# A split-float32 gated MLP with top-k masking on one Trainium2 core: the second of four token blocks takes the seven-product form of the shared down projection, and GpSimd multiplies by the magnitudes earlier

## The reference, cut to what matters

```python
xn = layernorm(x)                                   # x: 4 x 512 tokens of 1024 features
# part 1: gated MLP, 2752 units, half of them set to zero for each token
s = silu(xn @ w_gate.T)                             # 2752 columns
s = where(|s| is among the k = 1376 smallest of its row, 0, s)
part1 = (s * (xn @ w_up.T)) @ w_down.T
# part 2: squared-ReLU MLP ("shared", 2048 units) and one linear path ("routed", 512)
h = relu(xn @ up_w) ** 2
shared = h @ down_w                                 # 2048 -> 1024
routed = ((xn @ fc1_w) @ expert_w) * (sum of the 2 largest of xn @ gate_w) @ fc2_w
y = x + part1 + layernorm(shared + routed) * ln_gamma + ln_beta
```

## Time and profile before

| | us |
|---|---|
| median of 3 runs | 2283.11 (2279.87 to 2283.51) |
| profiled execution, its own time | 2282.36 |
| span of that execution's instructions | 2280.1 |
| TensorE busy in the span | 2263.9 (99%) |
| VectorE, ScalarE, GpSimd busy | 1327.3, 751.3, 939.2 |
| mean share of the DMA engines, from 637.07 MB | 79.9% |

### The profile page before, as it was taken

The page is one execution under the profiler, slowest core; times in us unless marked ns, Lnnn a source line. Parts: engine busy times, 40 slices in busy tenths (PEclk is TensorE's granted clock), DMA queues, the critical chain, the costliest instruction groups (busy, mean ns, idle before and its releaser), DMA issues.

```text
span 2280.1 us, 27377 instructions
## 1 busy us (share of the span) xinstructions
PE 2263.9 (99%) x10264; PEld 1882.5 (83%) x10264; DVE 1327.3 (58%) x1712; ACT 751.3 (33%) x1173; POOL 939.2 (41%) x670
## 2 busy tenths in 40 slices
PE   8999999999999999999999999999999999999999
PEld 6888888888888888888888888888788888888877
DVE  4332678757334456937434446788943543888870
ACT  3233654133334325301114334623112432551310
POOL 5456557487444523044014461136403455043620
PEclk9999999999999999999999999999999999999999
DMA  6799999788888878887678887668677888676955
GB/s 257 278 389 395 354 366 354 264 341 299 292 297 280 273 278 312 295 292 289 213 233 296 272 278 284 213 228 288 239 251 248 268 283 309 216 231 226 333 186 177
DMA packets 229158, 637.07 MB, mean 279 GB/s; under 512 B 23712, under 2 KB 32928, under 8 KB 225952
## 3 DMA queue, kind: packets, MB, share of 16 engines
q1 hardware_dynamic: 229024, 635.30, 79.9%
HBM read 483.10 MB, written 152.11 MB: 279 GB/s over the span
## 4 chain that ended last, share of the span: by engine, by line
PE 92%; DVE 3%; DMA 2%; SPq 1%; POOL 1%; ACT 1%; issue 0%; DVEq 0%; ACTq 0%
PE bank L1330 30%; PE bank L1332 30%; PE bank L1331 30%; PE bank L1350 1%; DMA mixed_w<-mixes 1%; DVE prod L1925 1%; DMA split_w<-w 1%; PE bank L1341 1%; SPq L800 0%; POOL w L1061 0%; SPq L796 0%; DVE prod_t L2061 0%; DVEq L1491 0%; PE bank L1430 0%; PE bank L1431 0%
## 5 line engine op out<-in xcount | busy, mean ns | idle before, releaser
L1061 POOL TENSOR_TENSOR w<-raw,w 128x512 fp32r<-128x512 f32 (+1 forms) x196 | 282.3, 1447 | 195.0 <-ACT w L1107 194.6
L1066 POOL TENSOR_TENSOR w<-w 128x512 fp32r<-128x512 f32 x146 | 214.5, 1496 | 199.1 <-ACT w L1284 199.0
L1330 PE MATMUL bank<-w,prod_t 128*128 128x512 f32 x672 | 269.5, 401 | 3.0 <-DVE prod_t L2061 3.0
L1332 PE MATMUL bank<-w,prod_t 128*128 128x512 f32 x672 | 262.9, 391 | 0.0
L1331 PE MATMUL bank<-w,prod_t 128*128 128x512 f32 x672 | 261.9, 390 | 0.0
L1330 PE MATMUL bank<-w,tok 128*128 128x512 f32 (+1 forms) x664 | 252.8, 381 | 0.7 <-ACT mag L1218 0.5
L1331 PE MATMUL bank<-w,tok 128*128 128x512 f32 (+1 forms) x664 | 252.0, 380 | 0.0
L1332 PE MATMUL bank<-w,tok 128*128 128x512 f32 (+1 forms) x664 | 252.0, 379 | 0.0
L1330 PE MATMUL bank<-tok,w 128*128 128x512 f32 x640 | 249.0, 389 | 0.0
L1331 PE MATMUL bank<-tok,w 128*128 128x512 f32 x640 | 249.0, 389 | 0.0
L1332 PE MATMUL bank<-tok,w 128*128 128x512 f32 x640 | 249.0, 389 | 0.0
(11 more groups left out here) (222 smaller groups left out, 4633.7 us busy)
## 6 DMA issues: line engine op xcount, KB each, us to landing
w<-split_w SPq DMA_DIRECT2D x448, 512.0 KB, 4.5
split_w<-w SPq DMA_DIRECT2D x184, 512.0 KB, 6.2
w<-mixed_w SPq DMA_DIRECT2D x176, 256.0 KB, 3.2
w_more<-split_w SPq DMA_DIRECT2D x88, 512.0 KB, 5.1
w_more<-mixed_w SPq DMA_DIRECT2D x128, 256.0 KB, 3.7
rows<-x_dram SPq DMA_DIRECT2D x32, 512.0 KB, 5.0
mixed_w<-own SPq DMA_DIRECT2D x12, 1024.0 KB, 6.8
spilled_u<-prod SPq DMA_DIRECT2D x12, 1024.0 KB, 8.0
```

The lines of the kernel that those rows point to most:

```text
L1061: pool.tensor_tensor(lo, words, hi, ALU.subtract).then_inc(lo_ready, 1)
L1066: pool.tensor_tensor(slot_of(g)[:, 1, :], slot_of(g)[:, 1, :].bitcast(F32), slot_of(g)[:, 0, :], ALU.subtract).then_inc(pool_lo, 1)
L1330: pe.matmul(out, left[0], right[0], start=first, stop=False)
L1332: return pe.matmul(out, left[1], right[0], start=False, stop=last)
```

## The change

It does three things. (1) `WIDE` becomes true for block 1, which so takes the order of a wide block and the seven-product form for pairs 5 and 6. (2) The eight sets of these pairs are made elsewhere: sets 20 to 23 in block 0 by VectorE, in a new buffer `first_own` over the search's scratch (loads from granules 148, 158, 176 and 192, mixing at +7, store at +8), and sets 24 to 27 in block 1 by GpSimd in `shared_own` (two loads at a granule and two at the next, from 152, 158, 165 and 172; mixing at +3; store at +5). (3) In wide blocks GpSimd multiplies chunks 0 to 15 of `prod` by `mag` before they are spilled (granules 148 to 151, four instructions of 128x2048), in place of sixteen of 128x512 behind out 0's masks; TensorE's turns then wait for the mask itself. The spills stand at 151, 153, 155 and 157.

```diff
-WIDE = [False, False, True, True]
+WIDE = [False, True, True, True]
...
+            if wide:
+                self.spill_at = {second + 4 + 2 * c: c for c in range(4)}
+                self.weigh_at = {second + 1 + c: c for c in range(4)}
...
         if wide:
-            for c in range(6):
-                del self.gated_at[out0 - TURN_LEAD + c]
+            self.gated_at = {}
             self.gated_at.update({begun + 6 + c: c for c in range(6)})
...
-SHARED_FROM = {n: 158 + 7 * i for i, n in enumerate(SHARED_SETS)}
-SHARED_LOADS = {at + i: (n, i) for n, at in SHARED_FROM.items() for i in range(4)}
-SHARED_AT = {at + 5: n for n, at in SHARED_FROM.items()}
-SHARED_STORES = {at + 6: n for n, at in SHARED_FROM.items()}
+FIRST_SHARED, SECOND_SHARED = SHARED_SETS[:HALF], SHARED_SETS[HALF:]
+SHARED_FROM = [dict(zip(FIRST_SHARED, (148, 158, 176, 192))), dict(zip(SECOND_SHARED, (152, 158, 165, 172)))]
+SHARED_LOADS = [{at + i: [(n, i)] for n, at in SHARED_FROM[0].items() for i in range(4)},
+                {at + i: [(n, 2 * i), (n, 2 * i + 1)] for n, at in SHARED_FROM[1].items() for i in range(2)}]
+SHARED_AT = [{at + 7: n for n, at in SHARED_FROM[0].items()}, {at + 3: n for n, at in SHARED_FROM[1].items()}]
+SHARED_STORES = [{at + 8: n for n, at in SHARED_FROM[0].items()}, {at + 5: n for n, at in SHARED_FROM[1].items()}]
...
+        first_own = over("first_own", [P, 4, N], F32, more_at + 2 * HID * 4)
...
             def load_shared_mix(n, i):
-                if n > SHARED_SETS[0]:
+                if n == FIRST_SHARED[0]:
+                    sp.wait_ge(masked, TILES)
+                elif n != SECOND_SHARED[0]:
                     sp.wait_ge(shared_stored, 16 * (n - SHARED_SETS[0]))
...
             def spill(b, c):
-                sp.wait_ge(up_signed, SIGNED.index((b, c)) + 1)
+                if WIDE[b]:
+                    sp.wait_ge(weighed, weighings(b, c) + 1)
+                else:
+                    sp.wait_ge(up_signed, SIGNED.index((b, c)) + 1)
...
+            def mix_second_shared(n):
+                ...                                  # the four subtractions, on GpSimd
...
+                    if m in plan.weigh_at:
+                        c = plan.weigh_at[m]
+                        ks = slice(4 * c, 4 * c + 4)
+                        pool.wait_ge(up_signed, SIGNED.index((b, c)) + 1)
+                        pool.tensor_tensor(prod[:, ks, :, :], prod[:, ks, :, :], mag[:, ks, :, :],
+                                           ALU.mult).then_inc(weighed, 1)
...
             def upper_early_sum(b, n):
                 act.wait_ge(unit_summed, shared_round(b, n) * UNIT_SUMS + 1)
+                if b == 1 and n == 0:
+                    act.wait_ge(shared_stored, 16 * len(SHARED_SETS))
...
             def turn_product(b, i):
-                pe.wait_ge(prod_ready, b * GK + i + 1)
+                if WIDE[b] and i >= TAIL_CHUNKS:
+                    pe.wait_ge(masked, (b * GC + GROUPS.index(c // 4) + 1) * TILES)
+                else:
+                    pe.wait_ge(prod_ready, prods(b, i) + 1)
```

More of the change, by code:

```diff
@@ L171, in __init__ @@
         self.late_hi_at, self.units_lo_at, self.units_cut_at = {}, {}, {}
+        self.weigh_at = {}
         shared_end = end["fast", SHARED_PAIRS[1], 6] if wide else end[("shared", 3)]
@@ L513, in unit_lo, with weighings, prods @@
     return len(names) * shared_round(b, n) + names.index(what) + 1
+def weighings(b, c):
+    return 4 * WIDE[:b].count(True) + c
+def prods(b, i):
+    return sum(TAIL_CHUNKS if wide else GK for wide in WIDE[:b]) + i
+TAIL_CHUNKS = 6
 SIGNED = [(b, g) for b in range(1, BLOCKS) for g in (GC - 2, 0, 1, 2, 3)]
@@ L724, in program @@
         prod_ready = sem("prod_ready")
+        weighed = sem("weighed")
         norm_step = sem("norm_step")
@@ L776, in late_place, with shared_place @@
             return raw_more[:, i, :]
+        def shared_place(n):
+            return first_own if n in FIRST_SHARED else shared_own
         def results_of(name):
@@ L841, in load_shared_mix @@
                 src, width = words_of((PAIRS[p][i // 2], k + i % 2 * HALF))
-                sp.dma_start(shared_own[:, i, :], src).then_inc(shared_loaded, 16)
+                sp.dma_start(shared_place(n)[:, i, :], src).then_inc(shared_loaded, 16)
             def store_shared_mix(n):
                 sp.wait_ge(shared_mixes, 4 * (n - SHARED_SETS[0]) + 4)
-                sp.dma_start(mixed_w[n].rearrange("i p n -> p i n"), shared_own[:, :, :]).then_inc(shared_stored, 16)
+                sp.dma_start(mixed_w[n].rearrange("i p n -> p i n"), shared_place(n)[:, :, :]).then_inc(shared_stored, 16)
             def load_norm(b):
@@ L870, in load_slot @@
                     sp.wait_ge(apply_step, b * 4 * TILES)
+                    if b == 1:
+                        sp.wait_ge(shared_stored, 16 * len(FIRST_SHARED))
                 for n, p in enumerate(SHARED_PAIRS):
@@ L931, in other_loads @@
                     store_own_mix(OWN_STORES[m])
[L932 to L935, removed]
+                if b < 2:
+                    for n, i in SHARED_LOADS[b].get(m, []):
+                        load_shared_mix(n, i)
+                    if m in SHARED_STORES[b]:
+                        store_shared_mix(SHARED_STORES[b][m])
                 if m == (plan.norm_load if b else FIRST_NORM_LOAD):
@@ L1033, in lower_early @@
                                    ALU.subtract).then_inc(early_lo, 1)
+            def mix_second_shared(n):
+                b11, b21, b12, b22 = (shared_own[:, i, :] for i in range(4))
+                at = 4 * (n - SHARED_SETS[0])
+                pool.wait_ge(shared_loaded, 64 * (n - SHARED_SETS[0] + 1))
+                pool.tensor_tensor(b11, b12, b11, ALU.subtract).then_inc(shared_mixes, 1)
+                pool.tensor_tensor(b12, b22, b12, ALU.subtract).then_inc(shared_mixes, 1)
+                pool.wait_ge(shared_mixes, at + 1)
+                pool.tensor_tensor(b22, b22, b11, ALU.subtract).then_inc(shared_mixes, 1)
+                pool.wait_ge(shared_mixes, at + 3)
+                pool.tensor_tensor(b21, b21, b22, ALU.subtract).then_inc(shared_mixes, 1)
             def late_mix(n):
@@ L1070, in _ @@
                             sum_lo(b, SUMS_LO_AT[b][m], j)
+                    if b == 1 and m in SHARED_AT[1]:
+                        mix_second_shared(SHARED_AT[1][m])
                     if m in plan.units_lo_at:
@@ L1564, in mix_own, with mix_first_shared @@
                 dve.tensor_tensor(b21, b21, b22, ALU.subtract).then_inc(own_mixes, 1)
-            def mix_shared(n):
-                b11, b21, b12, b22 = (shared_own[:, i, :] for i in range(4))
+            def mix_first_shared(n):
+                b11, b21, b12, b22 = (first_own[:, i, :] for i in range(4))
                 at = 4 * (n - SHARED_SETS[0])
@@ L1991, in _ @@
                                           ALU.subtract).then_inc(vector_lo, 1)
-                    if b == 1 and m in SHARED_AT:
-                        mix_shared(SHARED_AT[m])
+                    if b == 0 and m in SHARED_AT[0]:
+                        mix_first_shared(SHARED_AT[0][m])
                     if m in plan.units_at:
```

## The result

The changed kernel takes 2288.24 us (median of 10 runs, 2285.1 to 2289.93) against 2281.83 before (10 runs, 2279.87 to 2286.73): ratio 1.0028, 95% interval 1.002 to 1.0036, slower by 0.28%. The forecast was 2286.5, with 2277 to 2292 as the range. The profiled execution took 2289.93 us, the longest of the ten, with a span of 2288.1; so the differences of the traces come to 8.0 us where the medians differ by 6.4. By the line that the prediction drew (above 2287.7) this is slower.

A forecast was written before the change was run, and what follows sets the result against it. TensorE, busy 2263.9 of 2280.1 us, was taken as the bound. Terms -8.2 - 5.1 + 13.2 + 3.5 = +3.4 us took the profiled 2282.36 to 2285.8, or 2286.5 with 0.75 to the median; range 2277 to 2292.

The forecast's parts named there:

- Part 1: Block 1 in the wide form: 48 fewer matmuls make it as short as block 2, own waits apart; -8.2 us.
- Part 2: Products ahead of the spill: both waits in out 0 go, 1.7 us in each of three wide blocks; -5.1 us.
- Part 3: Block 1: ScalarE's wait for set 27's store delays count, pick, `cut_units` and A12; +13.2 us, within 11.9 and 15.
- The steps behind the store: Block 1, after set 27's store goes: landing, `upper_early_sum` (1.0 us), count (2.7 later), then the pick (7.1).
- So 1472.2 to 1475; I take 1473.5: Block 1, in block 2's times: when set 27's store goes, at some 17.5 us a set against 19.0 scheduled.
- Part 4: Block 0: the moved sets' DMA traffic makes TensorE wait for `w` between 455 and 480 us; +3.5, within 1.3 and 6.
- Sets 22 and 23 ... I take them as hidden: Block 0: these sets come 20 and more granules later, without `own`'s loads beside them, and were taken as hidden.
- that out 0 still waits: Sign of a wrong prediction: waits remain in out 0, where none for `prod_t` were foreseen in blocks 2 and 3.
- The clock fell: Rival, slower, 0.07: TensorE's clock falls in block 1's long wait; 2 us added if again or lasting, 2288.5.
- The wait was not hidden: Rival, faster, 0.10, held that block 1's ScalarE wait for set 27's store is hidden; about 2273 us.
- the products' move did what it says: Rival, 0.05, held that the products' move does nothing: out 0's waits stay, 3.4 to 5.1 us not won; 2291.
- Block 0 was not bound by DMA: Rival, slower, 0.10, held that block 0 becomes DMA-bound for longer, with 6 to 8 us remaining; about 2291.

The follow-up runs named there:

- r9: Changed kernel with S3 and S4 exchanged in their buffer and sets 24 to 27 started earlier in block 1 (148, 155, 162, 169): 2273.73 us, ratio 0.9966.
- r1: Kernel before with only the products' move (GpSimd multiplies chunks 0 to 15 of `prod` ahead of the spill, two wide blocks): 2277.48 us, ratio 0.9981.
- r3: Changed kernel with `upper_early_sum` one granule later in ScalarE's order, behind the search's last count: 2282.05 us, ratio 1.0001.
- r4: Changed kernel with S3 and S4 exchanged in their buffer, so `upper_early_sum` no longer waits for set 27's store: 2277.45 us, ratio 0.998.
- r7: Changed kernel with sets 24 to 27 started at granules 148, 155, 162 and 169 of block 1: 2281.2 us, ratio 0.9998.
- r5: Changed kernel with A11's lo word made two granules earlier on GpSimd, ahead of set 27's mixing in block 1: 2288.66 us, ratio 1.0029.
- r6: Changed kernel with S3 and S4 exchanged in their buffer and A11's lo word ahead of set 27's mixing on GpSimd: 2277.81 us, ratio 0.9987.
- r2: Changed kernel with `WIDE` false for block 1 again, the moved sets and products kept: 2287.26 us, ratio 1.003.
- r10: r9 without VectorE's subtractions for sets 20 to 23 in block 0, all loads and stores kept, results wrong: 2268.3 us, ratio 0.9948.
- r12: r9 with set 22 loaded from granule 180 and mixed at 190, behind out 0's last lo word, set 23 from 194 and at 201: 2271.07 us, ratio 0.9957.
- r8: Changed kernel with sets 22 and 23 loaded from granules 190 and 200 of block 0, so set 22 is mixed in out 1: 2290.76 us, ratio 1.0043.

## Why the forecast held, and where its steps did not

**Part 1 (-8.2)** held: with the waits taken out (r9) block 1 is 548.2 - 557.3 = -9.1 us. Without the products' -2.0 and without the 1.2 that it still has over block 2, that is -8.3. This is one trace against another, with the scatter said above.

**Part 2 (-5.1)** held, and was a little more: 2.0 a block instead of 1.7, in r1 too. The cause is as read: the masks take 2.73 us for four, 6.38 beside GpSimd. The Trainium skill's "SBUF — State Buffer", "Who interferes with whom", says that a VectorE instruction with two SBUF inputs contends with a GpSimd instruction that reads SBUF; these rows agree. The two sign products of granules 151 and 152, with GpSimd busy for about half of their time, took 4.78 us and not the 9 that I had allowed. Nothing waits for the search there, as foreseen. Whether the later spills, which run beside set 24's store in block 1, cost that block anything, no run separates.

**Part 3 (+13.2)** was the right mechanism, mis-sized: 18.1, outside the 11.9 to 15 given for it. That the count stands behind the wait is shown by r3, that the store is what is waited for by r4 and r7, and that it is one chain by r5. The steps behind the store were right within 0.6 us: 4.4 until it landed (I took 5.0), 3.7 for the two rows (3.7), 6.95 for the pick (7.1). The step that failed is "So 1472.2 to 1475; I take 1473.5", on this block's scale (S3 T3 due at 929.3 here, 1482.40 there) 920.4; the store went at 925.64, 5.2 us later. Set 24's store went at 865.67, some 1.5 us behind its granule, and set 25's loads went 8.6 us behind it, not 5, with the two last spills beside: by then the sets were over 7 us late. And from one store to the next, sets 26 and 27 took not 17.5 but 19.3 and 18.6 us, so the 19.0 us of schedule gave next to nothing back. r7 shows both: the first store went 12.4 us earlier and the last 10.1, the rest lost beside the spills.

A11's wait I had not seen at all: set 27's mixing stands ahead of A11's lo word. It cost nothing, as the same chain was later anyway (r5), but it is what remains when the chain is cut (r4), and then SP's queue (r6). A list of what stands behind each wait on GpSimd and SP, not on ScalarE alone, would have given both.

**Part 4 (+3.5)** was near in size and wrong in place and cause. From granule 156 to its end block 0 loses 6.4 us in the changed kernel's trace, and 4.0 to 5.5 in the seven others with the same program, r2 to r7 and r9; that the end of the block showed 4.4 is the 2.0 us won before. The loss is not between 455 and 480 us: the DMA engines are full there, and TensorE is busy all the time (the columns behind POOL's are the clock, the share of the DMA engines, and GB/s).

```profile
449.00:470.00 21.00, 21.00 (x94) 17.43 (x93) 15.26 (x20) 4.31 (x7) 8.58 (x6) 1.00 1.04 410
```

"Sets 22 and 23 ... I take them as hidden" is the step that failed. Set 22 is mixed in out 0, where VectorE stands for its loads and then lets `prod_t` wait; with the slow restarts, this is 4.0 of the 6.4 us (r10 and r12; r8 too, for the waits themselves). The two waits for `w` are the other 2.3. In r8 and r12, with the sets' work later, new waits for `w` came in out 1 and took back all or half of what was won. What makes the words of `w` late is open: r10, with all the traffic, has none of these waits, and no run takes SP's and GpSimd's rows there apart. One of the prediction's own signs of being wrong, that out 0 still waits, is thus there in block 0, though not in the wide blocks for which it was meant.

**The rivals.** The clock fell, and twice, but each time TensorE still had to wait for the chain behind it: it cost nothing. Where the chain is cut (r4) it costs about 1.5 us. The wait was not hidden, and the products' move did what it says. Block 0 was not bound by DMA: TensorE ran without a wait through the stretch where the engines were full, and r10 lost nothing with the same traffic.

**The sum.** In the traces: -8.2 (part 1) - 6.0 + 18.1 + 4.4 = +8.3, against 8.0 of the spans and +3.4 foreseen. By the medians the change is +6.4, almost double the +3.4. That the time still came within 1.7 us of the 2286.5 is in part luck: the forecast started from 2283.11, the median of three runs, where that of ten is 2281.83. Part 3 alone was 4.9 us too low.

## To carry to other kernels

A wait that is put in an in-order queue costs what stands behind it. Look at each engine's rows behind it, and move what does not need it ahead (r3), or give the buffer another place (r4). A chain of load, mix and store whose every step takes as long as the schedule gives it makes up no delay: what holds up its first link is paid at its last (r7). An instruction of VectorE that may have to wait for a load can cost more than its own length, if the engine's next product is waited for: put it where that is not so (r12), and look at what its transfers meet there (r8).

## What was unexpected of the hardware

After waits of 4.0 and 9.4 us TensorE started at a granted clock of 0.52 and 0.51 (1.2 GHz) for some 3.3 and 3.7 us, and was at 1.00 (2.4 GHz) behind that; the wait of 1.3 us in block 0 had no such trace (1.00 in the 3.3 us behind it). The windows of the changed kernel (the granted clock is the column behind POOL's):

```profile
928.00:931.30 3.30, 3.29 (x8) 2.66 (x9) 0.00 (x0) 1.30 (x2) 0.17 (x1) 0.52 0.42 153
931.50:935.00 3.50, 3.50 (x17) 2.71 (x15) 1.18 (x4) 2.19 (x2) 2.03 (x1) 1.00 0.11 14
944.60:948.30 3.70, 3.68 (x9) 2.91 (x10) 3.65 (x3) 2.24 (x5) 3.70 (x3) 0.51 0.08 32
948.50:951.80 3.30, 3.30 (x16) 2.59 (x14) 3.20 (x7) 0.78 (x1) 0.15 (x1) 1.00 0.54 164
```

That a long enough idle gap sends the clock back is what the Trainium skill's "TensorE: Matmul & The Clock Gate", "HAM oscillation — how this bites in real kernels", says; these rows agree. The subtractions of 128x512 on VectorE took 0.68 us with GpSimd idle and 1.5 to 1.8 beside it: the mixing in out 0 took 6.6 us, where four at 0.68 would be 2.7 (an estimate).
